# Linear attention on Trainium2: four heads' scores side by side on 32-row groups, the batches unrolled, and an inverse root taken as a power on POOL

## What is computed

```
q, k, v = proj(wq), proj(wk), proj(wv)                     # (4, 16, 256, 16)
q = (q @ fq1_w.T + fq1_b) * (q @ fq2_w.T + fq2_b)
k = (k @ fk1_w.T + fk1_b) * (k @ fk2_w.T + fk2_b)
inter = einsum(q * scale, cumulated k v of earlier chunks of 64)
s = where(tril, (q * scale) @ k.T, 0); intra = s @ v        # within a chunk
o = inter + intra
o = o * rsqrt(mean(o * o, axis=-1) + 1e-5) * norm_w         # per head
x = layernorm(x + o @ wo.T)
```

## Time and profile before

| | |
|---|---|
| median of three runs | 1167.86 us |
| the profiled execution | 1171.16 us, span 1169.3 us, mean granted clock 0.967 |
| PE, DVE, ACT, POOL busy over the span | 89%, 62%, 43%, 34% |
| the stage that is changed | start to 140.76 us, 12% of the span |
| instructions | 20911 |

### The profile page before, as it was taken

One profiled execution on the slowest core, in us unless ns is written; L12 is line 12 of the kernel. 1 busy time (PEld: TensorE's weight loads), 2 busy tenths in 40 slices (PEclk: granted clock), 3 DMA queues, 4 the chain that ended last, 5 costly groups with the idle time before them and its releaser, 6 DMA issues. The chain is left out here.

```text
span 1169.3 us, 20911 instructions
## 1 busy us (share of the span) xinstructions
PE 1038.2 (89%) x7242; PEld 841.5 (72%) x7242; DVE 723.1 (62%) x1496; ACT 503.0 (43%) x1091; POOL 396.5 (34%) x419
## 2 busy tenths in 40 slices
PE   9999998989699999999999789898998974999980
PEld 6676665666488888888888468687887832899980
DVE  2454667767744444456444658787877842688855
ACT  3424134444344544555444334343343441566640
POOL 3000050000166666666664134453444406000005
PEclk9999999999999999999999899999999987899995
DMA  4000010000323333333331101000000045755613
GB/s 161 1 1 0 0 27 1 2 0 0 131 83 113 104 112 101 99 101 96 113 105 54 41 1 42 1 18 22 18 22 18 0 136 213 274 197 211 222 36 109
DMA packets 55927, 87.33 MB, mean 75 GB/s; under 512 B 4784, under 2 KB 46000, under 8 KB 53680
## 3 DMA queue, kind: packets, MB, share of 16 engines
q1 hardware_dynamic: 54320, 82.19, 21.5%
q0 software_dynamic: 1536, 4.20, 1.1%
HBM read 75.36 MB, written 11.01 MB: 74 GB/s over the span
## 5 line engine op out<-in xcount | busy, mean ns | idle before, releaser
L1493 ACT ACTIVATE e_probs<-ps,e_neg_max 128x128 f32<-128x128 f32 (+1 forms) x128 | 52.8, 417 | 112.7 <-DVE e_neg_max L1440 112.7
L129 PE MATMUL ps<-warm 128*128 128x512 bf16 x358 | 90.7, 411 | 11.5 <-PEq L960 2.8
L1051 DVE TENSOR_TENSOR d_s_m<-ps,d_decay 128x768 f32<-128x768 f32 x64 | 58.3, 952 | 58.8 <-PE ps L1213 58.8
L120 PE MATMUL ps<-xTl,d_wh 128*128 128x512 f32 x192 | 80.2, 418 | 0.0
L129 PEld LDWEIGHTS ps<-warm 128*128 128x128 bf16 x358 | 36.6, 104 | 57.6 <-issue 24.1
L120 PE MATMUL ps<-xTh,d_wl 128*128 128x512 f32 x192 | 76.5, 399 | 0.0
L120 PE MATMUL ps<-xTh,d_wh 128*128 128x512 f32 x192 | 76.4, 398 | 0.0
L120 PE MATMUL ps<-wl_gated,f_wh 128*128 128x256 f32 x240 | 69.8, 291 | 3.1 <-DVE wl_gated L1792 2.0
L755 ACT ACTIVATE g_probs<-ps,g_neg_max 128x128 f32<-128x128 f32 (+1 forms) x128 | 46.9, 417 | 55.7 <-DVE g_neg_max L711 55.4
L120 PE MATMUL ps<-wh_gated,f_wh 128*128 128x256 f32 x240 | 68.3, 285 | 0.0
L120 PE MATMUL ps<-wh_gated,f_wl 128*128 128x256 f32 x240 | 68.2, 284 | 0.0
(11 more groups left out here) (362 smaller groups left out, 3366.7 us busy)
## 6 DMA issues: line engine op xcount, KB each, us to landing
f_stage<-in_w_experts SPq DMA_DIRECT2D x15, 1536.0 KB, 6.6
d_decay<-in_decay SPq DMA_DIRECT2D x32, 384.0 KB, 3.6
d_stage<-in_w_decay SPq DMA_DIRECT2D x32, 256.0 KB, 2.9
d_stage<-in_w_decay SPq DMA_DIRECT2D x32, 128.5 KB, 3.5
d_stage_v<-in_w_decay SPq DMA_DIRECT2D x32, 128.0 KB, 2.3
d_stage<-in_w_decay SPq DMA_DIRECT2D x32, 128.0 KB, 2.2
slot_rows<-warm SPq DMA_DIRECT2D x1, 3840.0 KB, 13.2
slot_outs<-f_rows SPq DMA_DIRECT2D x15, 256.0 KB, 2.1
```

Source lines behind the costliest of these rows:

```text
L120: mm = pe.matmul(out, w(k), x(k), start=(n == 0), stop=(n == 3 * len(ks) - 1))
L129: pe.matmul(out, c.warm16[:, 0:P], c.warm16[:, 0:out.shape[1]], start=True, stop=True)
L1051: dve.tensor_tensor(s_m[:, s % 2, 2 * b:2 * b + 2, :], ps[:, 2 + 2 * b:4 + 2 * b, 0:CAUSAL], decay[:], ALU.mult).then_inc(sm_ready, 1)
L1493: act.activation(probs[:, t % 4, cols], bank[:, cols], ACT.Exp, bias=neg_max[:, t % 4, b:b + 1], accum_out=sums[:, t % 4, b:b + 1]).then_i ...
```

## The change

It does four things in `layer0_linear_attention`.

1. *Scores by row groups.* `q_rows` and its copies are gone. The two parities of `q_par` and `k_map` are used by groups of 32 rows: group g of `q_par[par, m]` has one head that isn't zero. Four heads' products lie on four row groups and go to banks 2 to 5, with one semaphore for the four. A quad is now the heads of one parity and one half of the features. `q_par` and `k_map` have two buffers, `s_m` five quads.
2. *Masks by pairs of banks.* One DVE instruction masks two heads (128x768), with the triangle read twice. The values read v without padding, 16 columns a head.
3. *The loop is unrolled.* The four batches stand one behind the other, the maps of the next batch and the end of the last woven in; the projections of the first half, maps of batch 0 and projections of the second half alternate. The filler is gone from between the batches, and 10 and 3 stand in the last.
4. *The power.* POOL computes the mean square to the power -0.5 with one two-input instruction of 128x32 in place of ACT's root and DVE's reciprocal. The weighing by norm_w moves from DVE to ACT.

```diff
@@ pool
-            pool.memset(v_pad[:], 0.0).then_inc(zeroed, 1)
-            pool.memset(q_rows[:], 0.0).then_inc(zeroed, 1)
+            pool.memset(half_power[:], -0.5).then_inc(zeroed, 1)
...
+            for b in range(BATCH):
+                pool.wait_ge(var_ready, b + 1)
+                pool.tensor_tensor(stat[:, 3, :], stat[:, 1, :], half_power[:].broadcast_to((P, TPB * H0)), ALU.pow).then_inc(r_ready, 1)
@@ vector
-                    for h in range(4 * quad, 4 * quad + 4):
-                        dve.wait_ge(s_ps, LEAD + H0 * at(u) + h + 1)
-                        dve.wait_ge(pv_ps, LEAD + QUADS * at(u) + quad - 1)
-                        dve.tensor_tensor(s_m[:, h % 8, :], ps[:, 3 + h % 4, 0:CAUSAL], c.tri, ALU.mult).then_inc(sm_ready, 1)
+                n = QUADS * b + quad
+                dve.wait_ge(s_ps, n + 1)
+                need(dve, pv_ps, n - KEPT + 1)
+                for two in range(2):
+                    dve.tensor_tensor(s_m[:, n % KEPT, 2 * two:2 * two + 2, :], ps[:, 2 + 2 * two:4 + 2 * two, 0:CAUSAL],
+                                      c.tri.unsqueeze(1).broadcast_to((P, 2, CAUSAL)), ALU.mult).then_inc(sm_ready, 1)
...
-                    dve.wait_ge(sd_ready, LEAD + at(u) + 1)
-                    dve.reciprocal(stat[:, 3, :], stat[:, 2, :]).then_inc(r_ready, 1)
-                    dve.wait_ge(r_ready, LEAD + at(u) + 1)
+                dve.wait_ge(r_ready, b + 1)
+                need(dve, on_turned, b)
...
+            for b in range(BATCH):
+                masks(b, 0)
+                if b >= 2:
+                    add(b - 2)
+                masks(b, 1)
+                if b >= 1:
+                    moments(b - 1)
+                if b >= 1:
+                    scale(b - 1)
+                if b + 1 < BATCH:
+                    queries(b + 1)
+                masks(b, 2)
+                masks(b, 3)
+                if b + 1 < BATCH:
+                    keys(b + 1)
@@ scalar
-                    for g in range(4):
-                        rows = slice(32 * g, 32 * g + 32)
-                        act.activation(q_rows[rows, 2 * g:2 * g + 2].rearrange("p h k s -> p (h k s)"), q_par[rows].rearrange("p h k s -> p (h k s)"),
-                                       ACT.Copy).then_inc(qrows_ready, 1)
...
+            def weigh(b):
+                act.wait_ge(on_turned, b + 1)
+                need(act, wo_ps, b)
+                act.activation(o_nT[:].rearrange("p k s -> p (k s)"), ps[:, 7, :], ACT.Copy, scale=vecs[:, 4:5]).then_inc(oT_ready, 1)
@@ tensor
+            def scores(b, quad):
+                par, m = quad // 2, quad % 2
+                n = QUADS * b + quad
+                if quad == 0:
+                    pe.wait_ge(q_ready, 2 * b + 2)
+                    pe.wait_ge(k_ready, b + 1)
+                need(pe, sm_ready, 2 * n)
+                groups = [(ps[:, 2 + g, :], slice(ROWS * g, ROWS * (g + 1))) for g in range(4)]
+                for bank, rows in groups:
+                    pe.matmul(bank[:, 0:SEQ], k_map[rows, b % 2, m, 0:P], q_par[rows, b % 2, par, m, :], start=True, stop=True)
+                for bank, rows in groups:
+                    mm = pe.matmul(bank[:, SEQ:CAUSAL], k_map[rows, b % 2, m, P:SEQ], q_par[rows, b % 2, par, m, P:SEQ], start=True, stop=True)
+                mm.then_inc(s_ps, 1)
...
+            for b in range(BATCH):
+                scores(b, 0)
+                if b >= 1:
+                    values(b - 1, 2)
+                    values(b - 1, 3)
+                if b >= 2:
+                    project_out(b - 2)
+                scores(b, 1)
+                if b >= 1:
+                    turn(b - 1)
+                if b + 1 < BATCH:
+                    map_in(b + 1, Q)
+                scores(b, 2)
+                scores(b, 3)
+                if b + 1 < BATCH:
+                    map_in(b + 1, K)
+                if b >= 1:
+                    turn_back(b - 1)
+                values(b, 0)
+                values(b, 1)
```

More of the change, by code:

```diff
@@ new lines, in keys, with masks @@
+            def keys(b):
+                dve.wait_ge(map_ps, 2 * b + 2)
+                dve.wait_ge(second_k, b + 1)
+                dve.scalar_tensor_tensor(k_map[:, b % 2].rearrange("p k s -> p (k s)"), ps[:, 0, :], vecs[:, 2:3],
+                                         second[:, 2], ALU.add, ALU.mult).then_inc(k_ready, 1)
+            def masks(b, quad):
+                n = QUADS * b + quad
[4 more added lines that the diff above has]
+                                      c.tri.unsqueeze(1).broadcast_to((P, 2, CAUSAL)), ALU.mult).then_inc(sm_ready, 1)
@@ L287, in _ @@
+            moments(BATCH - 1)
+            scale(BATCH - 1)
+            add(BATCH - 1)
         @block.scalar
         def _(act):
-            give_lead(act, act_sems)
             for n in range(2):
@@ new lines, in projected, with second_queries @@
+            def projected(n):
+                kind, half, m = order[n]
+                act.wait_ge(p_ps, n + 1)
+                if kind == V:
+                    dst = v_all[:, 4 * half + 2 * m:4 * half + 2 * m + 2, :].rearrange("p t d -> p (t d)")
+                else:
+                    dst = (q_all, k_all)[kind][:, m, half * 512:(half + 1) * 512]
+                act.activation(dst, bank_of(n), ACT.Copy).then_inc(p_ready, 1)
+            def second_queries(b):
+                act.wait_ge(map_ps, 2 * b + 1)
+                need(act, q_ready, 2 * b)
+                for par in range(2):
+                    act.activation(second[:, par], ps[:, 1, :], ACT.Identity, bias=par_bias[:, par:par + 1],
+                                   scale=c.parity[:, par:par + 1]).then_inc(second_q, 1)
@@ new lines, in second_keys, with output, squares @@
+            def second_keys(b):
+                act.wait_ge(map_ps, 2 * b + 2)
+                need(act, k_ready, b)
+                act.activation(second[:, 2], ps[:, 1, :], ACT.Identity, bias=vecs[:, 3:4]).then_inc(second_k, 1)
+            def output(b, half):
+                act.wait_ge(pv_ps, QUADS * b + 2 * half + 2)
+                need(act, o_turned, TPB * b)
+                act.activation(o_sb[:, half, :], ps[:, 6 + half, :], ACT.Copy).then_inc(o_ready, 1)
+            def squares(b):
+                need(act, sum_ready, b)
+                for t in range(TPB):
+                    act.wait_ge(o_turned, TPB * b + t + 1)
+                    act.activation(o_sq[:, t, :].rearrange("p (a g d) -> p a g d", a=2, d=HD0), spread(t), ACT.Square).then_inc(sq_ready, 1)
@@ L458, in normalise @@
+            last = BATCH - 1
+            values(last, 2)
+            values(last, 3)
+            project_out(last - 1)
+            turn(last)
+            keep_warm(c, pe, ps[:, 5, :], 10)
+            turn_back(last)
+            keep_warm(c, pe, ps[:, 5, :], 3)
+            project_out(last)
 def normalise(c, tag, src, dst, rms=False, turned=None, weight=None, store=False, following=None, rms_too=None):
```

349 lines of the change are left out of this document (142 added, 207 removed).

## The result

The changed kernel takes **1162.83 us**, the median of 19 runs (1158.87 to 1169.36); the kernel before, beside it, 1169.92 (1165.38 to 1173.99, 19 runs). The ratio is 0.9947, with a 95% interval of 0.993 to 0.9963: faster by 0.5%, where 2.4% were forecast. The time lies outside the range given, above its end of 1151.

The account below looks back on a forecast made before the run. PE was taken as the bound, with scores, then waits between batches. The stage's 104.7 us against 140.8 saves 36.1, less 8.5 for the clock: 27.6, forecasting 1140.3 us from a median of 1167.86; range 1127.5 to 1151.

Parts of the forecast that it names:

- Moments and power: Each batch's statistics: sum and variance 0.90 us, POOL's power 1.29 (1.4 with handoffs), scaling 0.7.
- the sum: First stage's path at full clock: 30.1 + 14.0 + 16.3 + 17.4 + 26.9 = 104.7 us, against 140.8.
- a power costs sixteen simple elements: POOL's power on 128x32 priced like the simple instruction on 128x512: 1.29 us.
- The upper bound: For one power, POOL's longest arithmetic instruction in the trace, 128x1568: 3.58 us.
- POOL's power is slow: Rival: software power holds DVE's queue; 3.6 to 8.2 us gives 1149 to 1168 (chance 0.06), longer is slower (0.06).
- first scores: Start of the first batch's scores on PE: 30.1 us instead of 35.36.
- the masks of a quad: DVE's two 128x768 instructions for four heads: 1.82 us, 1.75 without what overlaps the next.
- The rival at the page's factor: Four row tiles gain 3.07, so a quad of scores takes 0.85 us; sum 3.1 us higher; chance 0.13.
- two quads of values: PE's value products after the scores in a batch: 1.44 us.
- The next stage's table load: ACT's load for the next stage's Sqrt, 1.28 us, lies within a 9.88 us wait and costs nothing.
- The clock: PE's clock falls to half rate when idle in the first stage, giving back 5 x 1.7 = 8.5 us.
- five falls of 3.42 us: One clock fall in each of four batches and one more, each costing up to half of 3.42 us.

Follow-up runs that it names:

- experiment 4: The changed kernel with POOL multiplying in place of raising to a power, output not normalised: 1137.75 us, a single run.
- experiment 7: The changed kernel with each batch's power split into two instructions of 128x16, DVE waiting for both: 1164.98 us, a single run.
- Experiment 6: The changed kernel with POOL raising to the power twice for each batch: 1185.0 us, a single run.
- experiment 5: The changed kernel with ACT's root and DVE's reciprocal back and filler (10, then 12 matmuls) before each batch's fourth scores: 1137.28 us, ratio 0.9712 to the kernel before.
- experiment 2: The changed kernel, power kept, with filler (10, then 30 matmuls) before each batch's fourth scores: 1157.07 us, ratio 0.9899 to the kernel before.
- experiment 1: The changed kernel with ACT's root and DVE's reciprocal back in place of POOL's power: 1143.88 us, ratio 0.9789 to the kernel before.
- experiment 3: The changed kernel, power kept, with DVE scaling a batch after the next one's last two quads of masks: 1150.35 us, ratio 0.9841 to the kernel before.

## Why the prediction was wrong, step by step

**The step that failed is "Moments and power", and in it one term: the power, mis-sized.** I took 1.29 us, with handoffs 1.4, and gave 0.22 and 3.58 as bounds; it is 5.43, with handoffs 5.53 to 5.57, so that it lies above its own upper bound. Four of them are 4 x (5.54 - 1.4) = 16.6 us of the 20.0 that the stage is late. By the sum such a power gives 1140.3 + 16.6 = 1156.9, 5.9 below the time measured; 3.4 of that (20.0 - 16.6) lie in the stage, nearly all of it the low clock (see the account below), and 2.1 are that the kernel before had 1169.92 beside the change and not 1167.86. The reasoning behind the 1.29 was "a power costs sixteen simple elements". By experiments 4 and 7 it costs 0.158 us an element (from two sizes), where a product costs (1287 - 240) / (512 - 32) = 2.2 ns (experiment 4's row against the earlier trace rows): 72 times as much. The upper bound was worse founded than the value: the longest arithmetic instruction that happens to stand in the trace bounds nothing that works by another method. The Trainium skill ("GPSIMD Engine Reference", section "3.1 Elementwise — side-by-side cycle accounting") counts about 2.6 cycles an element for a two-input add, and gives 4497 ns for 2048 elements, by my estimate 2.2 ns each. The product here agrees, with its 2.2 ns; the power is far from it.

**The mechanism was right, and stood among the rivals.** "POOL's power is slow" named the software, the element at a time and the queue behind the wait, with 1149 to 1168 us for a power between 3.6 and 8.2. Measured were 5.43 and 1162.8. It had a chance of 0.06, because I weighed 12 us against a product's price; no row of the trace spoke against 5 us. Experiment 6 shows its other end: 10.8 us a batch make the kernel slower. Between the two profiles (7.6 us of stage gained at 5.43, 14.6 lost at 10.8) the gain ends near 7.3 us a power, an estimate, where the rival said 8.2.

**The path.** With the clock held (experiment 5) the batches can be set against the sum, whose 1.4 is 0.65 there. From first scores to first scores the sum then says 14.0, 15.6 and 16.7 us, and 25.4 for the last; measured were 16.0 (29.45 to 45.49), 15.7, 17.0 and 25.1. Three are within 0.4 us. The first is 2.0 over, and 1.5 in experiment 2 (30.07 to 45.52). Most of that is the clock once more. The first filler stands behind the query map of this batch, and the map runs at the low clock:

```profile
33.37 3.46 PE L395 MATMUL ps<-a_q_all,a_maps 128*128 128x256 f32 x8
```

It takes 1.89 at full rate, so it is 1.6 longer here, and in experiment 2, with 3.05, 1.2 longer. ACT's second factors and DVE's query products wait for it. The other steps were near the sum: first scores at 30.21 (30.1 forecast); the masks of a quad 1.82; scores of a quad 0.71 and 0.40 like one head's. The rival at the page's factor needs a closer look than these durations. From its start to the start of the values behind it, a quad of the change takes 0.86 us, 0.10 over the sum's 0.76, where this rival had 0.20. Here is the last head of a quad in the kernel before, with the values behind it, and below it a quad of the change:

```profile
40.04 0.60 PE L391 MATMUL ps<-a_q_rows,a_k_map 128*128 128x256 f32 x2
40.48 0.38 PE L392 MATMUL ps<-a_q_rows,a_k_map 128*128 128x128 f32 x2
40.79 0.64 PE L403 MATMUL ps<-a_s_m,a_v_pad 128*32 128x256 f32 x8
```

```profile
47.52 0.71 PE L402 MATMUL ps<-a_q_par,a_k_map 32*128 32x256 f32 x8
48.05 0.40 PE L404 MATMUL ps<-a_q_par,a_k_map 32*128 32x128 f32 x8
48.38 0.62 PE L419 MATMUL ps<-a_s_m,a_v_all 128*16 128x256 f32 x8
```

The head takes 0.75 to the values' start, 0.10 over the 0.65 between heads, and a head behind values takes 0.10 more at its start too. So a single head between values would take 0.85, and four side by side take 0.86: the excess comes from changing work twice, of which the sum counted one, and not from the row groups. Over 16 quads it is at most 1.6 us, an estimate, and two quads of values, 1.31 instead of 1.44, take part of it back. The Trainium skill ("TensorE: Matmul & The Clock Gate", "Measured speedup vs the span model") gives 3.07 for four row tiles. The trace is near it when the quads are timed from values to values: four heads took 2.81 us from values to values before (41.58 to 44.40), 3.3 times a quad's 0.86. The next stage's table load, 1.28 us, lies beside DVE's statistics and cost nothing:

```profile
L590 ACT ACT_TABLE_LOAD x1 | 1.3, 1283 | 4.8 <-PEq L138 4.8
```

**The clock.** Forecast 8.5 us; filler gives back 8.5 with the power (experiment 2) and 8.2 without it (experiment 5 against 1). That the first of these hits the forecast is luck: the filler leaves out 1.9 us behind the last wait and 1.2 at the first query map, and with them the low clock costs about 11.6, an estimate. The picture was right only in part: I expected five falls of 3.42 us, there are six, and the stretches from 57 to 67 and from 81 to 91 us are low for 10 us each. Most of such a stretch is PE's wait for POOL and the masks (8.5 us), in which the low clock costs nothing; only the work behind it does.

**The account.** 16.6 (power) + 3.1 (low clock over the 8.5 forecast: 1.9 behind the last wait, 1.2 at the first query map) make 19.7 of the 20.0 us. The terms are read from profiles whose starts differ by up to 0.8 us, so that the sum comes so close is partly chance.

**What stays open.** From the last add to the end the ten profiled executions take 1024.7 to 1031.3 us, before 1028.5. The medians of experiments 1, 2, 3 and 5 gain 3 to 5 us less than their stages do (24.0 against 29.2 in experiment 1). Whether that is the profiled execution or something later in the kernel was not tried. It changes no verdict.

## What to carry to other kernels

Before an operation is moved to an engine that is free, find its price per element there: a bound must come from a row of the same operation, and without one the range has to reach the price at which the change loses, whatever simpler operations cost. Take a change apart when it makes two independent replacements: here everything but the power gave 29.2 us of stage, and the power gave 21.6 back to save two instructions that held DVE for 0.65 us a batch. And a wait in an in-order queue is charged with everything behind it: the same 5.43 us cost 13.8 us less in all when DVE asked for the result two quads later.

## What the runs showed of the hardware

- POOL's power: 5.43 us for 128x32 and 2.90 for 128x16, against 0.24 us for a product of 128x32 with the same operands. Two in a row take 5.42 and 5.41: the second is no cheaper.
- Four fp32 matmuls on 32 rows each, into four banks, take the time of one on 128 rows: 8 pieces of 256 columns in 0.71 us, 8 of 128 in 0.40, where one head's 2 take 0.70 and 0.38. A head's scores between values' rows take 0.10 us more on either side than between other heads.
- In this stage, where PE alternates with DVE, the mean granted clock from 27 to 110 us was 0.80 without filler and 0.98 with it, for 8.5 us of stage. Behind the last wait of 5.5 us, which 10 filler matmuls did not fill, 8 matmuls that take 1.99 us at full rate took 3.14.
- In the kernel before ACT loads a table four times in the stage, 1.28 us each, two of them ahead of a pass's second factors; without the root it loads none there, and each pass has its first scores 0.55 us sooner.
